# Shifting the tokens of the feed-forward block with TensorE transposes instead of a DMA between partitions

## The reference, cut to what matters

```python
def shift_tokens(t):
    a, s = jnp.split(t, 2, -1)                              # channels 0:64, 64:128
    s = jnp.pad(s, ((0, 0), (1, 0), (0, 0)))[:, :-1]        # second half from the token before
    return jnp.concatenate([a, s], -1)
def ffn_layer(x, g, bln, W1, b1, W2, b2):
    mu = x.mean(-1, keepdims=True)
    var = ((x - mu) ** 2).mean(-1, keepdims=True)
    xn = (x - mu) / jnp.sqrt(var + 1e-05) * g + bln
    hg = xn @ W1 + b1
    a, gate = jnp.split(hg, 2, -1)
    return a * jax.nn.gelu(gate, approximate=False) @ W2 + b2
for i in range(DEPTH):                                      # DEPTH = 6
    x = attn_layer(shift_tokens(x), Wqkv[i], q_scale[i], k_scale[i], Wo[i]) + x
    x = ffn_layer(shift_tokens(x), ln_g[i], ln_b[i], W1[i], b1[i], W2[i], b2[i]) + x
```

## Time and profile before

| | |
|---|---|
| median of 3 runs | 3772.14 us (3766.78 to 3774.6) |
| the profiled execution's own time | 3774.6 us |
| its span, first to last instruction | 3772.8 us |
| TensorE busy | 3613.5 us (96% of the span) |
| VectorE, ScalarE, GpSimd busy | 3193.1, 2811.2, 2403.1 us |
| mean granted TensorE clock | 0.984 of full speed |

### The profile page before, as it was taken

The page is one execution under the profiler, slowest core; times in us unless marked ns, Lnnn a source line. Parts: engine busy times, 40 slices in busy tenths (PEclk is TensorE's granted clock), DMA queues, the critical chain, the costliest instruction groups (busy, mean ns, idle before and its releaser), DMA issues.

```text
span 3772.8 us, 160639 instructions
## 1 busy us (share of the span) xinstructions
PE 3613.5 (96%) x70220; PEld 2629.1 (70%) x70220; DVE 3193.1 (85%) x4678; ACT 2811.2 (75%) x4978; POOL 2403.1 (64%) x1986
## 2 busy tenths in 40 slices
PE   7999999959999999999999999999999999999997
PEld 2222222247888888888888888888888888888885
DVE  7999999668888888888888888888888888888884
ACT  3888888847777777777777777777777777777773
POOL 3100000067787778878787787778777787778883
PEclk7999999979999999999999999999999999999998
DMA  4110000024434444444444444444444444444442
GB/s 119 38 41 19 23 21 20 2 76 129 114 107 111 118 128 108 110 117 117 123 107 115 119 111 115 120 118 111 111 114 124 116 111 109 133 122 108 112 108 60
DMA packets 210249, 366.46 MB, mean 97 GB/s; under 512 B 37107, under 2 KB 81735, under 8 KB 209223
## 3 DMA queue, kind: packets, MB, share of 16 engines
q1 hardware_dynamic: 209482, 355.05, 35.4%
HBM read 236.73 MB, written 111.67 MB: 92 GB/s over the span
## 4 chain that ended last, share of the span: by engine, by line
PE 66%; DVE 6%; issue 2%; ACT 2%; POOL 2%; DMA 0%; DVEq 0%; POOLq 0%; SPq 0%; ACTq 0%
PE PA L1302 14%; PE PB L1378 10%; PE PD L1391 9%; PE PD L1330 7%; PE PB L1302 5%; PE PC L1352 5%; PE PC L1416 3%; PE PC L1425 3%; PE PA L1361 3%; DVE T L1655 3%; PE PC L1409 3%; DVE T L1660 3%; ACT SQ L1497 1%; PE PD L1294 1%; PE PC L1346 1%
## 5 line engine op out<-in xcount | busy, mean ns | idle before, releaser
L1212 POOL TENSOR_TENSOR T<-T 128x1024 f32<-128x1024 f32 x384 | 908.8, 2379 | 26.3 <-DVE T L1660 26.3
L1230 POOL TENSOR_TENSOR T<-T,rn 128x1024 f32<-128x1024 f32 x384 | 731.7, 1906 | 27.1 <-POOL rn L1223 0.4
L1302 PE MATMUL PA<-Wqkv,XS 128*128 128x512 f32 x2304 | 635.5, 411 | 10.8 <-DVE XS L1621 7.9
L787 ACT ACTIVATE E<-p_low 128x512 f32<-128x512 f32 x1024 | 556.1, 597 | 115.4 <-PE p_low L637 101.2
L716 DVE TENSOR_REDUCE negmax<-p_max 128x1 f32<-128x1024 f32 x512 | 589.1, 1217 | 20.1 <-PE p_max L616 20.1
L1302 PEld LDWEIGHTS PA<-Wqkv,XS 128*128 128x128 f32 x2304 | 418.5, 195 | 82.3 <-DVE XS L1621 10.7
L1668 DVE TENSOR_REDUCE ss<-SQ 128x32 f32<-128x2048 f32 x192 | 437.0, 2276 | 0.0
L1378 PEld LDWEIGHTS PB<-ET,VW 64*64 64x64 f32 x24576 | 377.6, 135 | 56.7 <-DVE T L1660 29.5
L1378 PE MATMUL PB<-ET,VW 64*64 64x32 f32 x24576 | 399.7, 220 | 18.0 <-DVE T L1660 8.7
L1330 PE MATMUL PD<-ident,T 128*128 128x128 f32 x3072 | 409.4, 276 | 6.2 <-POOL T L1230 5.0
L1391 PEld LDWEIGHTS PD<-Wo,OT 128*128 128x128 f32 x3072 | 367.5, 193 | 61.9 <-issue 61.7
(11 more groups left out here) (158 smaller groups left out, 6560.7 us busy)
## 6 DMA issues: line engine op xcount, KB each, us to landing
VW<-v_rows SPq DMA_DIRECT2D x768, 256.0 KB, 4.5
v_rows<-Vs SPq DMA_DIRECT2D x192, 512.0 KB, 6.0
Wraw<-in_Wqkv SPq DMA_DIRECT2D x40, 192.0 KB, 5.8
QA<-parts_q SPq DMA_DIRECT2D x384, 16.0 KB
KA<-parts_k SPq DMA_DIRECT2D x192, 32.0 KB
fs<-XC SPq DMA_DIRECT2D x48, 127.0 KB
parts_q<-AO SPq DMA_DIRECT2D x8, 384.0 KB, 2.6
parts_k<-AO SPq DMA_DIRECT2D x8, 384.0 KB, 3.3
```

The costliest lines, as they stand in the source:

```text
L787: act.activation(E[:, s % 4, c, :], p_s[:, (64 * g + i) % NS, :], ACT.Exp, scale=DH ** -0.5)\
L1212: pool.tensor_tensor(out=t_, in0=t_, in1=T2[:, i * HALF:(i + 1) * HALF], op=ALU.add).then_inc(ad.sem, 1)
L1230: pool.tensor_tensor(out=t_, in0=t_, in1=rn[:, p, i * LH:(i + 1) * LH].unsqueeze(2).broadcast_to([P, LH, LD]), op=ALU.mult).then_inc(no.se ...
L1302: mm = pe.matmul(pair[:, half, :], XS[:, b, i, 1:P + 1], Wqkv[:, l % 2, j, lo:lo + 512], start=(k == 0), stop=(k == 2))
```

## The change

The token shift of the feed-forward block is done in transposed form. TensorE transposes the four tiles of X into PC[:, 0] (channels on partitions, tokens along the free dimension). ScalarE copies channels 0:64 to `FS[0:64, :, 0:128]` and channels 64:128 one column further, to `FS[64:128, :, 1:129]`; column 0 of the second half is carried over from column 128 of the step before, or is zero (`ff_carry`). TensorE transposes `FS[:, b, 0:128]` back into PC[:, 1], and VectorE copies that into `fx`. Statistics are taken over `fx`, and `ff_scale` works in place. XC, zrow, fs, `ff_rows`, `ff_keep` and the two DMAs of `shift` are gone.

```diff
--- before.py
+++ after.py
@@ -997,9 +997,7 @@
     VW = m.sb("VW", [P, 2, NW, 512])
     ET = m.sb("ET", [P, PAIRS, P])
     OT = m.sb("OT", [P, PAIRS, P])
-    XC = m.sb("XC", [P, 2, B, hc])
-    zrow = m.sb("zrow", [1, B, hc])
-    fs = m.sb("fs", [P, 2, B, hc])
+    FS = m.sb("FS", [P, B, P + 1])
     fx = m.sb("fx", [P, B, D])
     fst = m.sb("fst", [P, B, 6])
     fmv = m.sb("fmv", [P, B, 2])
@@ -1055,9 +1053,11 @@
     oe = m.count("l_oe")
     wo = m.count("l_wo")
     xd = m.count("l_x1")
-    xc = m.count("l_xc")
-    fk = m.count("l_fk")
-    fsh = m.count("l_fsh", 32)
+    f1 = m.count("l_f1")
+    f1e = m.count("l_f1e", 2)
+    fc = m.count("l_fc")
+    f2 = m.count("l_f2")
+    f2e = m.count("l_f2e")
     fsd = m.count("l_fst", 3)
     fr = m.count("l_frs")
     fn = m.count("l_fn")
@@ -1132,14 +1132,6 @@
                 for a in range(2):
                     lo = a * KW + c * WIN
                     sp.dma_start(VW[lo:lo + WIN, p, :, :], rows[:, :, a, :]).then_inc(vw[p].sem, 16)
-
-        def shift(u):
-            sp.wait_ge(xc.sem, xc.at(u))
-            if u > 0:
-                sp.wait_ge(fn.sem, fn.at(u - 1))
-            sp.dma_start(fs[1:P, 1, :, :], XC[0:P - 1, u % 2, :, :]).then_inc(fsh.sem, 16)
-            row = XC[P - 1:P, (u - 1) % 2, :, :] if u % NT else zrow[:, :, :]
-            sp.dma_start(fs[0:1, 1, :, :], row).then_inc(fsh.sem, 16)
 
         sp.wait_ge(s_one.sem, READY)
         for b in range(B):
@@ -1160,8 +1152,6 @@
             if d == 0 and u % NT == 2 and 0 < u // NT < NL:
                 sp.wait_ge(f5.sem, f5.at(u // NT * NT - 1))
                 load_ff(u // NT)
-            if d == 3 and is_step(u - 1):
-                shift(u - 1)
             if is_tile(s - 1):
                 values_in(s - 1)
             if is_tile(s):
@@ -1177,7 +1167,7 @@
     def on_pool(pool):
         pool.memset(power[:, :], -0.5).then_inc(s_one.sem, 1)
         pool.memset(kH[:, :, :, :], 0.0).then_inc(s_one.sem, 1)
-        pool.memset(zrow[:, :, :], 0.0).then_inc(s_one.sem, 1)
+        pool.memset(FS[:, :, :], 0.0).then_inc(s_one.sem, 1)
         lo = LASTW // 32 * 32
         pool.memset(zero[:, :], 0.0).then_inc(s_one.sem, 1)
         pool.memset(three[:, :], 1.5).then_inc(s_one.sem, 1)
@@ -1391,6 +1381,23 @@
                 mm = pe.matmul(PD[:, 0, 0:D], OT[:, j, :], Wo[:, l % 2, j, :], start=(j == 0), stop=(j == PAIRS - 1))
             mm.then_inc(wo.sem, 1)
             fd[0] = (xd.sem, xd.at(n))
+
+        def ff_shift(u):
+            pe.wait_ge(xd.sem, xd.at(B * u + B - 1))
+            free(fc_[0])
+            for b in range(B):
+                mm = pe.transpose(PC[:, 0, b * P:(b + 1) * P], X[:, b, u % NT, :], ident[:, :])
+            mm.then_inc(f1.sem, 1)
+            fc_[0] = (f1e.sem, f1e.at(u))
+
+        def ff_tokens(u):
+            pe.wait_ge(f1e.sem, f1e.at(u))
+            pe.wait_ge(fc.sem, fc.at(u))
+            free(fc_[1])
+            for b in range(B):
+                mm = pe.transpose(PC[:, 1, b * P:(b + 1) * P], FS[:, b, 0:P], ident[:, :])
+            mm.then_inc(f2.sem, 1)
+            fc_[1] = (f2e.sem, f2e.at(u))
 
         def ff_norm(u):
             pe.wait_ge(s_wf.sem, s_wf.at(u // NT))
@@ -1456,8 +1463,12 @@
                 attend(s - 3)
             if is_tile(s + 1):
                 input_T(s + 1)
+            if d == 3 and is_step(u - 1):
+                ff_shift(u - 1)
             if is_tile(s):
                 project_v(s)
+            if d == 3 and is_step(u - 1):
+                ff_tokens(u - 1)
             if d == 1 and is_step(u - 2):
                 ff_gate(u - 2, 0)
                 ff_gate(u - 2, 1)
@@ -1547,11 +1558,19 @@
             act.activation(kT[:, :, WIN:WIN + P], src, ACT.Copy).then_inc(te.sem, 1)
             act.activation(kH[:, n % B, :, :], src[:, :, P - WIN:P], ACT.Copy).then_inc(te.sem, 1)
 
-        def ff_keep(u):
-            act.wait_ge(xd.sem, xd.at(B * u + B - 1))
+        def ff_carry(u):
             if u > 0:
-                act.wait_ge(fn.sem, fn.at(u - 1))
-            act.activation(fs[:, 0, :, :], X[:, :, u % NT, 0:hc], ACT.Copy).then_inc(fk.sem, 1)
+                act.wait_ge(f2.sem, f2.at(u - 1))
+                act.wait_ge(f1e.sem, f1e.at(u - 1))
+            src = FS[hc:D, :, P:P + 1] if u % NT else zero[hc:D, :].unsqueeze(2)
+            act.activation(FS[hc:D, :, 0:1], src, ACT.Copy).then_inc(fc.sem, 1)
+
+        def ff_shift(u):
+            src = PC[:, 0, :].rearrange("p (b n) -> p b n", b=B)
+            act.wait_ge(fc.sem, fc.at(u))
+            act.wait_ge(f1.sem, f1.at(u))
+            act.activation(FS[0:hc, :, 0:P], src[0:hc], ACT.Copy).then_inc(f1e.sem, 1)
+            act.activation(FS[hc:D, :, 1:P + 1], src[hc:D], ACT.Copy).then_inc(f1e.sem, 1)
 
         def ff_norm(u):
             act.wait_ge(s_wf.sem, s_wf.at(u // NT))
@@ -1583,6 +1602,8 @@
                 ff_gate(u - 2, 1)
             if is_tile(s):
                 square(s, 0)
+            if d == 3 and is_step(u - 1):
+                ff_carry(u - 1)
             if d == 2 and is_step(u - 2):
                 ff_gate(u - 2, 2)
             if is_tile(s):
@@ -1597,7 +1618,7 @@
             if is_tile(s + 1):
                 input_T(s + 1)
             if d == 3 and is_step(u - 1):
-                ff_keep(u - 1)
+                ff_shift(u - 1)
             if d == 2 and 0 <= u < last * NT:
                 split_next(u)
             if is_tile(s - 3):
@@ -1674,17 +1695,16 @@
             dve.wait_ge(wo.sem, wo.at(n))
             dve.tensor_tensor(out=X[:, b, t, :], in0=PD[:, 0, 0:D], in1=X[:, b, t, :], op=ALU.add).then_inc(xd.sem, 1)
 
-        def ff_rows(u):
-            dve.wait_ge(xd.sem, xd.at(B * u + B - 1))
-            if u > 1:
-                dve.wait_ge(fsh.sem, fsh.at(u - 1))
-            dve.tensor_copy(XC[:, u % 2, :, :], X[:, :, u % NT, hc:D]).then_inc(xc.sem, 1)
+        def ff_tokens(u):
+            dve.wait_ge(f2.sem, f2.at(u))
+            if u > 0:
+                dve.wait_ge(f3.sem, f3.at(u - 1))
+            dve.tensor_copy(fx[:, :, :], PC[:, 1, :].rearrange("p (b n) -> p b n", b=B)).then_inc(f2e.sem, 1)
 
         def ff_stats(u):
-            dve.wait_ge(fk.sem, fk.at(u))
-            dve.wait_ge(fsh.sem, fsh.at(u))
+            dve.wait_ge(f2e.sem, f2e.at(u))
             for b in range(B):
-                i = dve.bn_stats(fst[:, b, :], fs[:, :, b, :])
+                i = dve.bn_stats(fst[:, b, :], fx[:, b, :])
             i.then_inc(fsd.sem, 1)
             dve.wait_ge(fsd.sem, fsd.at(u, 1))
             dve.memset(w["spare"][:, :], 0.0)
@@ -1696,11 +1716,9 @@
 
         def ff_scale(u):
             dve.wait_ge(fr.sem, fr.at(u))
-            if u > 0:
-                dve.wait_ge(f3.sem, f3.at(u - 1))
             for b in range(B):
-                i = dve.tensor_scalar(fx[:, b, :].rearrange("p (a c) -> p a c", a=2), fs[:, :, b, :],
-                                      fmv[:, b, 0:1], frs[:, b:b + 1], ALU.subtract, ALU.mult)
+                i = dve.tensor_scalar(fx[:, b, :], fx[:, b, :], fmv[:, b, 0:1], frs[:, b:b + 1],
+                                      ALU.subtract, ALU.mult)
             i.then_inc(fn.sem, 1)
 
         def ff_value(u, i):
@@ -1722,7 +1740,7 @@
 
         dve.wait_ge(s_one.sem, 6)
         for j in range(2):
-            dve.tensor_scalar_mul(XS[:, :, j, :], zero[:, :].unsqueeze(2).broadcast_to([P, B, P + 2]), 1.0)\
+            dve.tensor_scalar_mul(XS[:, :, j, :], FS[:, :, 0:1].broadcast_to([P, B, P + 2]), 1.0)\
                 .then_inc(s_one.sem, 1)
         dve.wait_ge(s_one.sem, READY)
         input_T(0)
@@ -1734,8 +1752,6 @@
                 ff_value(u - 2, 1)
             if is_tile(s - 4):
                 output(s - 4)
-            if d == 3 and is_step(u - 1):
-                ff_rows(u - 1)
             if d == 3 and is_step(u - 2):
                 ff_value(u - 2, 2)
             if is_tile(s):
```

## The result

The median is 3822.53 us (3810.43 to 3826.06, 4 runs) beside 3773.37 us before: ratio 1.0129, 95% interval 1.0106 to 1.0152. The change makes the kernel 49 us slower; forecast were 61 us, 3833 us, with a range from a little under 3813 to 3865 us. The profiled execution took 3821.91 us, with a span of 3820.1 us, 47.3 us more than before.

The account below looks back on a forecast made before the run. TensorE was taken to set the pace, busy 493.77 of 500 us. 1.35 us more per step, 47 x 1.35 = 63.5, minus 2.5 in the drain, gives +61 us on 3772.1: 3833 us, range 3813 to 3865.

Parts of the forecast that it names:

- What goes away costs nothing in a full step: Every full step: removing the copies into XC and fs and the shift's DMAs, all off the path, was counted as zero.
- The second group with its hand-over, 0.64 us: TensorE, slot d = 3: four transposes back from FS, followed by ff_down, cost 0.64 us a step.
- The first group, 0.44 us: TensorE, slot d = 3, between input_T and v projection: four transposes of X cost 4 x 0.109 = 0.44 us.
- The bank, 0.1 us of 0 to 0.2: Slot d = 3: ff_shift waits for VectorE to free PC[:, 0]; 0.1 us taken, between 0 and 0.2.
- ScalarE's copies, 0.2 of 0 to 0.6: Slot d = 3: TensorE's ff_tokens waits 0.2 us for ScalarE's two copies from PSUM; bounds nothing to 0.6 us.
- GpSimd's slack stays, because GpSimd moves by less than TensorE: Second normalising product before slot 0's transposes: 0.4 us of slack stays, with GpSimd 1.2 us late and TensorE 1.35.
- The drain, minus 2.5 us: Last step's chain: transposes and copies replace the 7.22 us DMA, 2.8 us earlier, of which 2.5 us were counted.
- Sum: Whole kernel: 47 x 1.35 = 63.5 us, minus 2.5, gives +61 us and 3833 us; chance 0.75.
- the uncovered round trip: Rival, slots 3 and 0: later copies or bank stall TensorE, 2.3 us a step, 3877 us; chance 0.12.
- The gap in the scores: Rival, slot 1's 0.6 us gap: a second per step gives 3861 us (chance 0.05), none gives 3805 (0.04).
- Gaps without a releaser in other slots: Sign in the profile after: TensorE gaps with no known releaser in other slots would show the prediction wrong; no size given.
- The clock: Rival, TensorE: added transposes bring the granted clock down, 1 us a step more, 3880 us; chance 0.02.

Follow-up runs that it names:

- the unread transposes: Kernel before plus two groups of four transposes of X in slot d = 3 that nobody reads, DMA shift kept: 3840.09 us, ratio 1.0191.
- the run without cover: Changed kernel with the first group of transposes moved behind the v projection, so nothing lies between the two groups: 3872.06 us, ratio 1.0278.
- `ff_scale` first: Kernel before plus eight transposes nobody reads, with VectorE's ff_scale moved ahead of ff_down in slot d = 3: 3803.09 us, ratio 1.0096.

## Why the prediction was right

The direction, the place and the mechanism were right: TensorE set the pace, the removed work had been hidden, and the added transposes lie in the open. Point by point:

- *What goes away costs nothing in a full step.* Nearly so, as the kernel without the shift shows: I counted zero and it was 0.05 us, read from the interval 2 to 3 (the steps, 60.54 against 60.56 us, can't tell so little).
- *The second group with its hand-over, 0.64 us*: it was 0.50. This is the mis-sized term, the whole of what 1.35 is above 1.22. I had taken the row of the `fx` transposes in front of the output projection, and `ff_down` follows closer (0.50 us in the changed kernel, 0.44 behind the unread transposes).
- *The first group, 0.44 us.* It was 0.38, and this made no difference, because ScalarE's copies end later than the v projection.
- *The bank, 0.1 us of 0 to 0.2*: 0.10, but the group began 0.27 us behind `input_T` and not at 0.17, since without any wait it begins 0.17 behind it and not 0.08. *ScalarE's copies, 0.2 of 0 to 0.6*: 0.15. The end of their chain, which sets the time, is where I had put it (the second group 2.28 us behind `input_T`; mine was 2421.2 - 2418.93 = 2.27), and in part by luck: the two copies took 1.21 us instead of 1.09, and the hand-over to TensorE 0.05 instead of 0.16. The extra ScalarE copy showed that there is no slack behind them.
- *GpSimd's slack stays, because GpSimd moves by less than TensorE.* It moved by more. Its second normalising product ends 13.28 us behind `input_T` instead of 11.97, so 1.31 us later against TensorE's 1.22, and the slack went from 0.4 us to 0.31. It was used up when VectorE was made later by one copy.
- *The drain, minus 2.5 us*: 2.7 in the change's profile, 3.2 in the kernel with the last step alone, 4.3 in the changed kernel's second profile. The sum behind it was off: I had charged 1.1 us for each group, and they took 0.63 and 0.66, so that the statistics start 3.5 us earlier and not 2.8. That 2.5 came near the first profile is luck with TensorE's clock: it was 0.61 under `ff_down` there, which took back 1.4 us of the 3.3.
- *Sum.* 47 x 1.22 = 57, less 47 x 0.05 and 2.7 in the drain gives 52 us; measured 49 and, in the second set of rounds, 50. The runs of one kernel spread over 9 to 16 us, so the remaining 2 to 3 us say nothing; in the two profiles, which differ by 47.3 us, the gap in `attend` alone is 2.4 us shorter after the change.

Of the rivals, the uncovered round trip did not come. What it costs when it does, the run without cover shows: 2.42 us a step and 104 us in all, close to the 2.3 and 105 that I had for it. The gap in the scores neither doubled nor went. "Gaps without a releaser in other slots", which I had put down as a sign of being wrong, are there, in `attend`, but the kernel before has more of them. The clock stayed at 1.00 in the full steps, and the figure of the Trainium skill ("TensorE: Matmul & The Clock Gate", Part 4: PE-mode transpose) of 275 ns for each transpose would have given 2.2 us a step for what cost 0.92 with the wait for the bank. What I had not listed is the case that the run with unread transposes fell into: the same work moved VectorE's scaling beside GpSimd's product and cost 0.6 us a step. In the changed kernel the scaling ends at 2452.25 + 1.24 = 2453.49 and GpSimd's product starts at 2453.55, so it missed this by 0.06 us in the slot I read, and by 0.06 or 0.07 in 40 of the 41 slots (0.34 in the other). That is no accident: both hang on GpSimd's power -0.5 there. The scaling starts 0.05 us behind the end of the power and lasts 1.24, and GpSimd has four small instructions to do, 1.35 us, before its product. In the kernel with unread transposes `ff_scale` hung on `ff_down` instead. I could have seen the danger in the trace of the kernel before. In its drain the scaling meets GpSimd's two closing products, and its four instructions take 3.14 us, where they take 1.23 in a full step:

```profile
3748.38 3.14 DVE L1702 TENSOR_SCALAR fx<-fs,fmv,frs 128x128 f32<-128x128 f32 x4 [0.55 <-POOL frs L1200]
```

```profile
3748.31 1.26 POOL L1242 TENSOR_TENSOR X<-X,gate_b 128x512 f32<-128x512 f32 x1
3749.66 1.26 POOL L1246 TENSOR_TENSOR X<-X,Wqkv 128x512 f32<-128x512 f32 x1
```

## What to carry to other kernels

Here, with TensorE busy for 98% of a step, all that was moved to it was paid, whatever it relieved, and the price was the pitch in the timeline with the hand-over behind it, not the recorded length. Where a second engine's chain ends last, as ScalarE's does here, its end sets the time, and what TensorE's own parts beneath it take counts no longer. Look at what becomes of a second engine's order when the first one's work shifts: a pair of VectorE and GpSimd instructions that come to lie side by side cost more here than half of the added work, and swapping two parts took it away. And the hidden DMA was the cheaper shift here: 0.05 us in a full step, and 7.22 us of latency once, in the drain, where it is on the path.

## What the runs showed of the hardware that was not expected

- `tensor_scalar` of 128x128 on VectorE, 0.34 us by itself, lasted up to 2062 ns beside a GpSimd product (2.06 beside one of 1.91 us, 1.93 beside one of 2.02); the mean of 164 was 750 ns.
- ScalarE's copy of 64 x 512 from PSUM takes 0.59 us, as long as one of 128 x 512 (0.60 us each, two in 1.09 us). Halving the partitions gained nothing here, and the two of the shift followed each other at 0.62 us, not at 0.49.
- A gap of 0.15 to 1.2 us in the middle of the scores of slot 1, nearly always after 54 of their 128 products, for which no releaser is recorded, came in nearly every step of every kernel here (26.8 us after the change, 19.2 with `ff_scale` first). A like gap of 0.2 to 1.1 us came in `attend` after 28 of 128, 5 times before, 4 times after the change and once in most of the other kernels. Their cause was not tried and stays open; together they are worth up to 31 us.
